# A four-layer sequence network: which of an instruction's waits is written first

## The reference

```python
x = L0(x)   # h = layernorm(x)*(1+scale)+shift, positions gathered by a table; x + gate * mamba(h)
x = L1(x)   # attention, 16 heads of 16, softmax over the keys; LN, silu, projection
x = L2(x)   # as L0, without the gather
x = L3(x)   # linear attention, softmax over q's head channels and over k's positions
# mamba(h): xz = h@W_in; u = silu(causal conv of 4 taps); dt = softplus(...); B, C from u@W_xp
#   for t: hst = hst*exp(dt_t*A) + (dt_t*u_t)*B_t ; y_t = sum_n hst[n]*C_t[n]   (512 channels, 16 states)
#   return ((y + u*D) * silu(z)) @ W_out
```

## Time and profile before

| | |
|---|---|
| median of 3 executions | 5507.8 us |
| the profiled execution | 5501.84 us, its span 5500.1 us |
| mean granted TensorE clock | 0.885 |
| busy: TensorE, VectorE, GpSimd, ScalarE | 83%, 84%, 74%, 59% |
| DMA, mean | 212 GB/s |

### The profile page before, as it was taken

How to read it: one execution, slowest core, us unless ns; L and a number is a source line. 1 busy time by engine, 2 the same in 40 slices (tenths; PEclk the granted TensorE clock), 3 DMA queues, 4 the chain that set the end, 5 groups by cost and what they waited for, 6 DMA issues and landing times.

```text
span 5500.1 us, 54997 instructions
## 1 busy us (share of the span) xinstructions
PE 4551.2 (83%) x16792; PEld 2433.0 (44%) x16792; DVE 4640.8 (84%) x4711; ACT 3256.8 (59%) x5572; POOL 4061.4 (74%) x2838
## 2 busy tenths in 40 slices
PE   4577888988889888888888888888988888888755
PEld 1243444444444444444454444444444444444423
DVE  2729899998999899999989999999989889999373
ACT  2335566666666666666666666666666666666252
POOL 1718787887878787887878788787878778787172
PEclk8668899999999899999999999999999899998775
DMA  4616666766766666676667667676667667666161
GB/s 147 215 46 230 221 233 223 238 231 221 245 216 233 223 235 225 223 248 216 234 217 237 220 230 237 219 246 210 236 221 240 219 221 248 219 230 219 37 208 53
DMA packets 355068, 1164.54 MB, mean 212 GB/s; under 512 B 39355, under 2 KB 79348, under 8 KB 354774
## 3 DMA queue, kind: packets, MB, share of 16 engines
q1 hardware_dynamic: 310614, 1106.42, 59.6%
q10 hardware_dynamic: 44160, 54.60, 3.1%
HBM read 1140.78 MB, written 20.10 MB: 211 GB/s over the span
## 4 chain that ended last, share of the span: by engine, by line
PE 41%; DVE 28%; issue 10%; POOL 9%; ACT 8%; DMA 3%; SPq 1%; DVEq 0%; ACTq 0%; POOLq 0%
DVE hw L1039 15%; PE ps L926 7%; DVE ps L1025 7%; PE ps L698 5%; PE ps L1231 5%; PE ps L1277 4%; POOL hw L1057 4%; PE ps L1304 3%; PE ps L1222 3%; PE ps L1320 2%; DVE mx L1397 2%; PE ps L707 2%; ACT da L975 2%; POOL hw L1064 2%; PE ps L669 1%
## 5 line engine op out<-in xcount | busy, mean ns | idle before, releaser
L1057 POOL TENSOR_TENSOR hw<-hw,cs 128x1024 f32<-128x1024 f32 x1024 | 2413.2, 2357 | 698.7 <-DVE hw L1039 636.2
L1039 DVE TENSOR_TENSOR_SCAN hw<-da,ps 128x1024 f32<-128x1024 f32 x1024 | 2335.4, 2281 | 94.9 <-ACT da L975 21.2
L975 ACT ACTIVATE da<-dt,a_neg 128x510 f32<-128x510 f32 x2048 | 1332.1, 711 | 193.7 <-DVE hw L1039 191.2
L1064 POOL TENSOR_TENSOR hw<-hw 128x512 f32<-128x512 f32 x1024 | 1297.9, 1267 | 66.3
L926 PE MATMUL ps<-hw,ident 128*128 128x512 f32 x2048 | 1184.0, 683 | 180.7 <-POOL hw L1064 180.6
L1025 DVE TENSOR_TENSOR ps<-ps,bs 128x1024 f32<-128x1024 f32 x1024 | 1256.6, 1227 | 67.0 <-DMA bs<-bc_scratch 7.1
L926 PEld LDWEIGHTS ps<-hw,ident 128*128 128x128 f32 x2048 | 399.9, 213 | 634.0 <-issue 322.6
L698 PE MATMUL ps<-hT,w_in 128*128 128x512 f32 x1024 | 534.5, 658 | 68.7 <-DVE dt L886 47.8
L1372 ACT ACTIVATE pts<-ps 128x512 f32<-128x512 f32 x512 | 278.5, 593 | 441.7 <-PE ps L1304 441.7
L1397 DVE TENSOR_REDUCE mx<-ps 128x2 f32<-128x512 f32 x512 | 332.0, 681 | 166.5 <-PE ps L1277 165.6
L1277 PE MATMUL ps<-k,q 32*128 32x256 f32 x2048 | 354.3, 469 | 112.5 <-DVE mx L1397 112.0
(11 more groups left out here) (178 smaller groups left out, 5306.8 us busy)
## 6 DMA issues: line engine op xcount, KB each, us to landing
bs<-bc_scratch SPq DMA_DIRECT2D x1024, 512.0 KB, 4.4
cs<-bc_scratch SPq DMA_DIRECT2D x1024, 512.0 KB, 4.9
taps<-taps_scratch SPq DMA_DIRECT2D x32, 512.0 KB, 5.5
xhat<-in_x ACTq DMA_DIRECT2D x16, 512.0 KB, 7.2
gate<-gates_scratch ACTq DMA_DIRECT2D x64, 128.0 KB, 5.2
x_b<-in_x ACTq DMA_DIRECT2D x16, 512.0 KB, 7.6
x_scratch<-x_b ACTq DMA_DIRECT2D x16, 512.0 KB, 3.4
x_c<-x_scratch ACTq DMA_DIRECT2D x16, 512.0 KB, 6.4
```

Source lines behind the costliest of these rows:

```text
L975: ins = nc.scalar.activation(da[q % (AHEAD + 1)][:, k, :, 1:S], dt_[:, c, :].rearrange("p (b s) -> p b s", b=GB)[:, :, 1:S], ACT.Exp, scal ...
L1039: nc.vector.tensor_tensor_scan(tile[:, :, :].rearrange("p n t -> p (n t)"), da[s % (AHEAD + 1)][:, :, :, :].rearrange("p n b s -> p (n b s)"),
L1057: nc.gpsimd.tensor_tensor(tile[:, :, :], tile[:, :, :], cs[s % C_RING][:, :, :], ALU.mult)\
L1064: nc.gpsimd.tensor_tensor(tile[:, 0, :], tile[:, 0, :], tile[:, 1, :], ALU.add)\
```

## The change

The order of the waits in front of four places in the code changes. Nothing else does: no instruction is added, removed or moved, and every instruction still has all its waits.

```diff
@@ scan_vector: dbx (L1025)
-                if s % PER == 0:
-                    dve.wait_ge(pc.of(f"dxp{c}"), pc.upto(g, f"dxp{c}"))
-                dve.wait_ge(*b_slice(l, g, s))
                 if s:
                     dve.wait_ge(pc.of(f"scan{s - 1}"), pc.upto(g, f"scan{s - 1}"))
                 elif before is not None:
                     kind, k = number(*before)
                     dve.wait_ge(kind.of(f"scan{STEPS - 1}"), kind.upto(k, f"scan{STEPS - 1}"))
+                if s % PER == 0:
+                    dve.wait_ge(pc.of(f"dxp{c}"), pc.upto(g, f"dxp{c}"))
+                dve.wait_ge(*b_slice(l, g, s))
@@ scan_vector: scan (L1039)
+                dve.wait_ge(pc.of(f"dbx{s}"), pc.upto(g, f"dbx{s}"))
                 dve.wait_ge(pc.of(f"exp{s}"), pc.upto(g, f"exp{s}"))
                 if s >= RING:
                     dve.wait_ge(pc.of(f"red{s - RING}"), pc.upto(g, f"red{s - RING}"))
...
-                dve.wait_ge(pc.of(f"dbx{s}"), pc.upto(g, f"dbx{s}"))
@@ times_c (L1057)
+            pool.wait_ge(pc.of(f"scan{s}"), pc.upto(g, f"scan{s}"))
             pool.wait_ge(*c_slice(l, g, s))
-            pool.wait_ge(pc.of(f"scan{s}"), pc.upto(g, f"scan{s}"))
@@ attn_tensor, both passes over the pairs (L1277, L1304)
-                for hh in range(2):
+                for hh in (1, 0):
```

## The result

The changed kernel takes 5465.32 us in the median of six executions (5456.22 to 5486.62); the kernel before, on the same chip, 5507.38 us (5499.19 to 5512.93, six executions). The ratio is 0.9926 with a 95% interval of 0.9907 to 0.9946: some 42 us or 0.7% faster. The profiled execution took 5456.22 us.

The account below looks back on a forecast made before the run. No engine was full, so waits between engines were taken to bound the kernel. 27.8 us saved less 5.8 paid left 22.0; three quarters, 16.5, gave 5507.8 - 16.5 = 5491 us, range 5477 to 5507.

Parts of the forecast that it names:

- The prices: Gaps per joint: VectorE 0.10 or 0.14 us to 0.03-0.04, GpSimd 0.14 to 0.08, TensorE's weight load 0.12 to 0.06.
- The sum on the chain: Bare joints on the chain at dbx, scan, multiplication and attention: 27.8 us saved, 5.8 us paid, net 22.0 us.
- What is paid: Moved waits that come last on the chain: decay 3.4 us, L989 1.5, C slice 0.7, B slice 0.2; together 5.8 us.
- As long as durations stay, that is a ceiling: Whole chain: at unchanged durations at most 22.0 us is gained, since the shortened old chain is still a path.
- The prediction's own sign for this: On TensorE: if matmul durations or the granted clock of 0.885 move, it was the clock.
- Three quarters of it: Whole kernel: of the net 22 us three quarters, 16.5 us, would show, because other paths lie beside the chain.
- Neighbours take over: TensorE's own path so near the chain that about a quarter of the gain is left: 5502 us; chance 0.16.
- VectorE pays anyway: Scan and dbx gaps come from the result's way, not the wait's place; 3.5 us gained, 5504 us; chance 0.06.
- the last wait is not the one chosen: At the reordered waits, those written first don't come last: nothing gained, 5.8 us paid, 5514 us; chance 0.05.
- TensorE's clock: One more idle stretch per group of two sequences lowers the granted clock, 52 us in all: 5544 us; chance 0.07.

Follow-up runs that it names:

- four separately timed parts: Waits of dbx, of the scan, of GpSimd's multiplication, of the attention loops, each reordered alone in the kernel before: ratios 0.9980, 0.9977, 0.9991, 0.9990.
- the whole: The changed kernel with all four reorderings, run again against the kernel before on one chip: 5454.83 us against 5502.12, ratio 0.9910.
- the scan alone: Only the waits in front of the scan (L1039) reordered, against the kernel before: 5485.41 us against 5498.27, ratio 0.9977.
- before + 112: The kernel before, waits untouched, with 112 unused matmuls added where TensorE waits: 5471.19 us against 5499.24, ratio 0.9954.
- the pair: Waits of dbx and of the scan reordered together, the rest as in the kernel before: 5481.17 us against 5502.12, ratio 0.9957.
- the other kernel: The changed kernel with waits reordered at more places, with 192 unused matmuls instead of 112: 5469.85 us against 5439.11.

## Why the prediction was wrong

- **The prices** of the gains were right: 0.03 and 0.04 us measured for the two joints of VectorE, 0.08 for GpSimd, 0.06 for the weight load. The pair in the earlier trace rows, the same instructions in both forms, was the row to trust.
- **The sum on the chain** came out in total: net 22.0 us counted, 22.6 us (6 either way) as the sum of four separately timed parts at equal clock, 24.4 us (5 either way) for the whole. Place by place it fits less well. The count has some 16 us in the 13 middle groups and 6 us in the other three. If TensorE's busy time is paid one for one, as in the two pairs of groups above, the joints gave some 7 us in the middle and at least 14 us in the other three. That is one profiled execution of each kernel, so an indication only, but the agreement of the total may be in part luck.
- **What is paid** was oversized for the decay: 0.06 us on the chain and not 0.10, so 34 x 0.06 = 2.0 us where 3.4 were counted. It was not tried by itself; the scan alone gave 8.4 us where 8.6 - 3.4 was counted.
- **"As long as durations stay, that is a ceiling"** is the step that failed. The durations did not stay. The same matmuls took 20 us less, and where both kernels' clocks are known execution by execution, 24 of the 48.7 us are left at equal clock. (For the first pair, 42 us apart, the clock of the kernel before is known only for the profiled execution.) The sum has no term for the clock, and the lower end of the range, 5480 - 3, was built on the 27.8 us of the joints alone. With about half of the gain outside the sum no care in the counting could have held it. The prediction's own sign for this, matmul durations or the granted clock moving from 0.885, came true.
- **Three quarters of it** fell too. The cut stood for neighbours that take over. They did, as the chain shows (VectorE 28 to 19 points), and yet the whole at equal clock is 24.4 us, not 16.5, which lies outside the 5 us either way. Whether joints off the old chain made up for it is not shown.
- **The rivals.** "Neighbours take over", "VectorE pays anyway" and "the last wait is not the one chosen" are excluded: the first by the 24.4 us at equal clock, the other two by the gaps. "TensorE's clock" named the right resource with the wrong sign: it weighed the clock as a risk (one more low stretch a group, 3.3 us each) and, against it, that the idle stretches get shorter, and did not draw from that very sentence that stretches of half clock might go away. It also read such a place as one in each group, 16 in all, where the trace has 143. And the earlier trace rows have a mean of 0.75 over 6.8 us, so about half of that stretch at half clock, which costs nearer 1.7 us than 3.3. The kernel before had groups of 310.6 and of 318.4 us with the same work, in plain sight in its trace. Its 13 middle groups were 4.0 us longer on average than the shortest of them, 52 us in all, which no term used.

**What stays open.** That the clock is worth tens of us here is shown (before + 112), and so is that the change, which touches nothing but waits, raised it (0.0058 on one chip). That it did so by shortening TensorE's waits is argued: the four parts, the pair and the whole all had a higher mean clock than their kernel before (0.8862, 0.8862, 0.8870, 0.8870, 0.8878, 0.8912 against 0.8854 to 0.8858), which fits, but no run holds the joints and moves only the lengths of the waits. Why the rise of the whole (0.0058) is more than that of its parts (0.0032 together, on another chip) is open as well.

## What to carry to other kernels

Where an instruction has several waits, write the one that comes last first, and price it by a pair in the trace that has both forms; count it on the chain, and don't discount the count without a row that says so. Before a ceiling is written down, look whether equal pieces of work in the trace of before take unequal time: here the spread between groups, at 0.91 and 0.93 of clock, was up to 8 us in a group, and adding up to 52 us it was larger than the effect in question. Compare small gains at equal granted clock as well as by the medians, or the parts will not add up.

## What was not expected of the hardware

- Where a wait is written is worth 0.06 to 0.10 us a joint: in an instruction of its own 0.10 us (one wait) and 0.14 us (two), carried by the waiting instruction 0.03 to 0.04 us, on VectorE. When the instruction in front has its waits fulfilled early, it costs nothing: in the kernel before, with other instructions between dbx and scan, L1404 the last, the scan starts even before the recorded end of that one, 2501.49 us:

```profile
2500.81 0.68 DVE L1404 TENSOR_TENSOR q<-q,ps 128x512 f32<-128x512 f32 x1
2501.40 2.28 DVE L1039 TENSOR_TENSOR_SCAN hw<-da,ps 128x1024 f32<-128x1024 f32 x1
```

- One kernel, one chip, 34 executions: 5487 to 5513 us, with a granted clock of 0.888 down to 0.883. Over 140 executions 4.2 us go with each 0.001.
- The granted clock is not low only where TensorE stands still for long: behind waits of 1.48 and 0.80 us for the maxima it was 0.50, and the 5.5 ms of the kernel before hold 143 such stretches.
- Matmuls that compute nothing, placed where TensorE waits, made the kernel before 0.5% faster, though TensorE was busy 69 us longer; the kernel's own matmuls took 57 us less; 80 more of them in the other kernel cost 31 us again.
